# A quantised decoder layer: a lighter prologue, the output codes without GpSimd, power-of-two scales in three steps, and layer norms split with ScalarE

## The reference

```python
# self attention, 16 heads of 64, everything quantised to 8 bits with power-of-two scales
s(t)  = exp2(ceil(log2(max|t| / 127)));  fq_floor(t) = clip(floor(t / s), -128, 127) * s
h     = layernorm(x) * fq_round(gamma) + fq_round(beta)
q,k,v = split(fq_floor(fq_floor(h) @ fq_round(w_qkv)))
dots  = fq_floor(q @ k.T * temp);  attn = fq_floor(softmax(dots))
out   = fq_floor(fq_floor(attn @ v) @ fq_round(w_out))
x1    = layernorm(x + out)                                  # post-norm
# linear cross attention: no softmax, so the context is used only through k.T @ v of each head
x2    = layernorm(x1 + (layernorm(q @ (k.T @ v) * scale + x1) * g + b))
# feed forward: W1, gelu, W2 with affine 8-bit activations and symmetric 8-bit weights
y     = layernorm(x2 + qlinear(gelu(qlinear(x2, W1, b1)), W2, b2))
```

## Time and profile before

| | us |
|---|---|
| three executions | 511.37, 513.91, 508.60 |
| median | 511.37 |
| the profiled execution, its own time | 509.18 |
| its span, from the first to the last instruction | 507.4 |
| around the span | 1.8 |

### The profile page before, as it was taken

How to read it: one execution, slowest core, us unless ns; L and a number is a source line. 1 busy time by engine, 2 the same in 40 slices (tenths; PEclk the granted TensorE clock), 3 DMA queues, 4 the chain that set the end, 5 groups by cost and what they waited for, 6 DMA issues and landing times.

```text
span 507.4 us, 7393 instructions
## 1 busy us (share of the span) xinstructions
PE 251.0 (49%) x1547; PEld 112.7 (22%) x1556; DVE 437.8 (86%) x1429; ACT 332.9 (66%) x739; POOL 174.3 (34%) x333
## 2 busy tenths in 40 slices
PE   0768766877767772222222222209995616405040
PEld 0644221421321211011111111103331614302030
DVE  4995899599769998999999999967775988987967
ACT  1013997299699992899999999954775622516230
POOL 7450000200030000588888888880000804430010
PEclk9976999589955555555555555558999675557557
DMA  7800000000134432188888888783004000000002
GB/s 261 211 2 0 0 0 0 1 21 21 43 116 173 184 146 104 37 191 190 191 189 190 191 188 186 166 165 43 2 1 125 16 1 1 0 1 0 0 1 83
DMA packets 85231, 43.65 MB, mean 86 GB/s; under 512 B 69064, under 2 KB 74456, under 8 KB 85083
## 3 DMA queue, kind: packets, MB, share of 16 engines
q1 hardware_dynamic: 83642, 43.21, 33.3%
q10 hardware_dynamic: 1568, 0.21, 0.3%
HBM read 8.28 MB, written 1.58 MB: 19 GB/s over the span
## 4 chain that ended last, share of the span: by engine, by line
DVE 53%; PE 25%; issue 13%; ACT 5%; DVEq 1%; DMA 1%; POOL 1%; ACTq 0%; SPq 0%
PE ps L476 24%; DVE mem L1176 11%; DVE mem L940 8%; DVE d_max L943 6%; DVE row_max L1176 2%; DVE m L1446 2%; DVE m L1447 2%; DVE mem L1321 2%; DVE mem L1086 1%; ACT mem L847 1%; DMA mem<-in_x 1%; DVE r_now L939 1%; DVE row_code L939 1%; DVE neg_max L939 1%; DVE m L943 1%
## 5 line engine op out<-in xcount | busy, mean ns | idle before, releaser
L476 PE MATMUL ps<-mem 64*128 64x256 bf16 (+6 forms) x1236 | 198.3, 368 | 141.6 <-DMA mem<-mem 83.7
L476 PEld LDWEIGHTS ps<-mem 64*128 64x128 bf16 (+5 forms) x1244 | 83.4, 130 | 252.3 <-issue 169.2
L847 ACT ACTIVATE mem<-mem,neg_max 128x256 f32<-128x256 int16 x256 | 126.3, 494 | 14.0 <-DVE neg_max L939 10.1
L1176 DVE CUSTOM_DVE_ANT_0 mem<-ps,fold,c 128x256 int16<-128x256 f32 x256 | 111.1, 470 | 0.0
L430 POOL TENSOR_SCALAR mem<-mem,r_now 128x256 int16<-128x256 f32 x176 | 80.9, 478 | 72.7 <-DVE r_now L939 72.7
L1086 DVE TENSOR_TENSOR mem<-mem 128x1024 bf16<-128x1024 bf16 x84 | 54.3, 683 | 14.8 <-ACT mem L799 14.7
L799 ACT ACTIVATE mem<-ps,c 128x1024 bf16<-128x1024 f32 x48 | 48.3, 1292 | 1.2 <-PE ps L476 1.2
L847 ACT ACTIVATION_READ_ACCUMULATOR mem<-mem,neg_max 128x1 f32 x256 | 47.8, 187 | 0.0
L813 ACT ACTIVATE mem<-ps,c 128x1024 int16<-128x1024 f32 x32 | 36.0, 1203 | 13.2 <-DVEq L1120 11.9
L940 DVE TENSOR_SCALAR mem<-mem,c 128x2048 bf16<-128x2048 int16 (+3 forms) x43 | 38.0, 895 | 6.4 <-PE ps L476 6.0
L430 POOL TENSOR_SCALAR fine_third<-mem,r_now 128x256 int16<-128x256 f32 x80 | 36.8, 478 | 5.0 <-DVE r_now L939 5.0
(11 more groups left out here) (201 smaller groups left out, 369.8 us busy)
## 6 DMA issues: line engine op xcount, KB each, us to landing
mem<-mem SPq DMA_DIRECT2D x64, 256.0 KB, 2.4
mem<-in_L_attn_w_qkv SPq DMA_DIRECT2D x1, 1536.0 KB, 9.9
mem<-in_L_attn_w_out SPq DMA_DIRECT2D x2, 512.0 KB, 10.8
out<-mem SPq DMA_DIRECT2D x4, 256.0 KB, 2.3
mem<-in_L_ffn_W SPq DMA_DIRECT2D x2, 256.0 KB, 6.0
xattn_matrix<-mem SPq DMA_DIRECT2D x1, 512.0 KB
mem<-xattn_matrix SPq DMA_DIRECT2D x1, 512.0 KB
mem<-mem SPq DMA_TRANSPOSE x22, 4.3
```

What stands on the lines that cost most here:

```text
L476: return te.matmul(o_, l_, r_, start=start, stop=stop)
L847: ins = sc.activation(e_ring[:, u % 4, pos], y_ring[:, u % 4, pos], ACT.Exp, scale=scale_reg, bias=neg_max[:, u % 4, pos:pos + 1], accum_o ...
L1176: ins = ve.tensor_tensor_reduce(y_ring[:, slot, pos], ps[:, 2 * slot + pos // 2, (pos % 2) * N:(pos % 2 + 1) * N], shift, col("g_dots"), - ...
```

## The change

In the prologue, x comes as two halves, the first on SP's queue and the second as the first DMA of ACT's queue, in rows of 1 KB (two neighbouring tokens on a partition; the output is stored the same way). `gbc` follows on ACT's queue, then the bias rows, then the weights. VectorE works out gamma's and beta's codes before the statistics. w_out, W1 and W2 aren't loaded or measured here, but once, late, behind the dots; their maxima, scales, codes and transposes are done between the groups of AV. The context gets a column of ones, so that the Gram matmuls give its sums too and GpSimd adds nothing. h and w_qkv are coded in halves and thirds, and the maximum pass starts with the first of them. `a1`, `r2`, `kv`, `xm` and `xbv` move behind the maximum pass and between units of the code pass, whose loops are written out. AV uses three double banks. `scale_of` works on the fp32 bits in three steps. VectorE reads the last AV pair in PSUM, bank by bank. GpSimd's casts of the output codes go to VectorE. In layer norms 1, 3 and 4 ScalarE normalises two tiles of each quarter, for which VectorE makes `nmr`, minus mean times factor; GpSimd's `x1_beta` waits for all quarters.

```diff
@@ sync: loads @@
-            sp.dma_start(x_in, x.rearrange("b (c p) d -> p (b c) d", p=P)).then_inc(sem("x_loaded"), 16)
+            sp.dma_start(x_in_pairs[:, halves[0]], x_pairs[:, halves[0]]).then_inc(sem("x_first"), 16)
             sp.dma_start(w_qkv_f, w_qkv).then_inc(sem("w_loaded"), 16)
...
-            sp.dma_start(w_out_again, w_out.rearrange("(j p) d -> p j d", p=P)).then_inc(sem("w_out_again"), 16)
+            sp.dma_start(w_out_f, w_out.rearrange("(j p) d -> p j d", p=P)).then_inc(sem("w_late"), 16)
+            sp.dma_start(w1_f, w1.rearrange("(c p) d -> p c d", p=P)).then_inc(sem("w_late"), 16)
+            sp.dma_start(w2_f, w2).then_inc(sem("w_late"), 16)
@@ scalar: loads @@
+            act.dma_start(x_in.rearrange("p (b c) d -> p b (c d)", c=2)[:, B // 2:B],
+                          x.rearrange("b (p c) d -> p b (c d)", c=2)[:, B // 2:B]).then_inc(sem("x_second"), 16)
             act.dma_start(gbc[:, 0:1], at_g[:, None]).then_inc(sem("gb_loaded"), 16)
             act.dma_start(gbc[:, 1:2], at_b[:, None]).then_inc(sem("gb_loaded"), 16)
+            act.dma_start(bkv[:, 0], x_bk[None, :].to_broadcast((B, D))).then_inc(sem("bkv_loaded"), 16)
@@ gpsimd @@
-            for bb in range(B // 2):
-                pool.wait_ge(sem("o_i_act"), bb + 1)
-                pl.tensor_scalar(o_cv[:, bb, 1], o_iv[:, bb, 1], 1.0, 0.0, ALU.mult, ALU.add)\
-                    .then_inc(sem("o_codes_odd"), 1)
@@ tensor: prologue, and between the units of the code pass @@
+            for b in range(4):
+                gram_of(b)
             pe.wait_ge(sem("xw_T"), 1)
+            across(6, diag6[:, 2:3], 1)
+            for b in range(4, 6):
+                gram_of(b)
+            across(0, diag, 1)
+            for b in range(6, B):
+                gram_of(b)
...
+            first = {1: ("hT_codes", 2), 2: ("gram_ready", 2), 3: ("gram_ready", 3), 8: ("w_codes", 3)}
...
+            a1_half(0)
+            across(5, diag, 1)
+            a1_half(1)
...
+                    if n == 4:
+                        pe.wait_ge(sem("a1_ready"), 1)
+                        kv_main(0)
+                    if n == 6:
+                        kv_bias(0)
...
+                    if n == 20:
+                        pe.wait_ge(sem("kv_ready"), 2)
+                        xm_half(0)
@@ vector @@
-                link(ts(t_, grown, factor, TINY * GROW, ALU.mult, ALU.max))
...
+                link(ts(s_out, grown, factor, TINY * GROW * HALF_RANGE, ALU.mult, ALU.max))
+                link(ts(bits, bits, 0x7F800000, None, ALU.bitwise_and))
+                link(ts(inv_out.bitcast(I32), bits, -1.0, float(0x7F000000), ALU.mult, ALU.add))
...
             dve.wait_ge(sem("gb_loaded"), 32)
             link(absmax(m6[:, 0:2], gbc[:].rearrange("p (k n) -> p k n", n=1)))
+            across_send(m6, 2, diag6)
+            across_take(2, 7, x6)
...
+                if grp == 3:
+                    dve.wait_ge(sem("w_late"), 48)
+                    absmax(m6[:, 3:4], w_out_f.rearrange("p j d -> p (j d)")).then_inc(sem("late_max"), 1)
...
+            for k in range(2):
+                dve.wait_ge(sem("av_group"), B * GROUPS - 1 + k)
+                absmax(d_max[:, k:k + 1], ps[:, last_bank + k, :]).then_inc(sem("o_last"), 1)
...
+            for bb in range(B // 2):
+                o_ints(bb)
+                if bb:
+                    o_odd(bb - 1)
+                o_even(bb)
+            o_odd(B // 2 - 1)
...
             def normalise(name, dst, src, q, done):
-                for t in range(4 * q, 4 * q + 4):
+                for t in range(4 * q, 4 * q + 2):
                     ins = norm(dst, src, t)
@@ scalar: layer norms @@
+            def norm_act(name, dst, src, q, done):
+                act.wait_ge(ln_sem(name, "shift"), ln_count(name, q))
+                for t in range(4 * q + 2, 4 * q + 4):
+                    ins = sc.activation(dst[:, t], src[:, t], ACT.Identity, scale=rsd[:, t:t + 1], bias=nmr[:, t:t + 1])
```

559 lines of the change are left out of this document (320 added, 239 removed).

## The result

The changed kernel takes 491.5 us (median of 4 runs, 490.66 to 491.69) against 510.99 for the kernel before (4 runs, 508.6 to 513.91): ratio 0.961, 95% interval 0.956 to 0.967. It is faster by 3.9%. The profiled execution took 491.34 us with a span of 489.4, so by its own time it is 17.8 shorter than the one before (509.18), by the span 18.0. One of the executions that follow, 512.95 us with the third norm on VectorE, ran at a granted clock of 0.58 where its neighbours had 0.68 to 0.70, and no median counts it.

The account below looks back on a forecast made before the run. Streams were taken as bound by two full engines, seams by chains everybody waits on; the change works on seams. Terms 10.0 + 4.0 + 0.9 - 1.5 + 5.7 + 2.5 + 1.3 = 22.9 from 509.18 gave 486.3; stated 487.5, range 478 to 498.

Parts of the forecast that it names:

- Prologue, 10.0: Start to the maximum pass's first matmul: statistics at 15.3, equivalent start at 39.8 instead of 49.83, gain 10.0 us.
- Passes, 4.0: Between, inside and behind the qkv passes: 1.4 + 1.1 - 2.2 - 2.5 + 6.2, gain 4.0 us.
- The term 1.4 for the start: Between the qkv passes: less fp32 work ahead of the exchange, so ScalarE's first code unit comes 1.4 us earlier.
- 1.1 - 2.2 - 2.5: Code pass: ScalarE's gap closed 1.1 us, its added copies cost 2.2, fp32 blocks starving it cost 2.5 (0 to 5).
- Shorter scales, 0.9 for two: Scales for dots and attention: two steps of 0.2 us saved, 0.45 each, gain 0.9 us.
- AV, -1.5: AV: a product of 384 fp32 columns and eight transposes put between TensorE's groups, loss 1.5 us.
- Last pair and output codes, 5.7: After AV: earlier last-pair reduction 0.85 us, scale 0.45 twice, output codes without GpSimd 3.95, gain 5.7.
- Norms 1 to 3, 2.5: Layer norms: first norm 0.8 us, third norm's split and better order before `sum3` 1.7; gain 2.5, between 0 and 5.
- Norm 4, 1.3: Fourth layer norm: 2.0 us less 0.7 at the end, gain 1.3, between 0 and 2.
- a load that isn't held up (481.5): Rival, prologue: `gbc` lands at 4.5, statistics at 9.5, 5.8 us less, 481.5; chance 0.12.
- the clock staying low (531): Rival: new fp32 blocks and late waits keep TensorE at 1.2 GHz through AV and the code pass, 531 us; chance 0.03.
- "Little comes" (495): Rival: GpSimd's products hold VectorE 2.6 us more, fp32 blocks starve the pass 2.5 more, norms give nothing: 495; chance 0.17.

## Why the prediction was right, and where its steps were off

The forecast was 487.5 with a range of 478 to 498; measured 491.5. The sign and the seams were right, and so were the two largest terms, prologue and output codes, within 2 us. The sum was 22.9 where the profiles show 18.0, and it is that near by some luck: four terms fell short by 7.2 in all, three came out 2.3 better. Term by term:

- **Prologue, 10.0: 8.1 came.** The statistics came at 17.45 for 15.3. Of that 1.4 is the load, in at 11.88 for 10.5, held by w_qkv as argued from the earlier trace rows: gamma ahead of w_qkv took 4.0, beta with it 8.4. The other 0.8 is GpSimd's hold, taken at 0.8 and found 1.6 here and up to 3.3, so its upper bound was right. From w_qkv's maximum to the first matmul it was 11.1 us for 11.8; the wait of 2.5 for TensorE in there did not come (the exchange at 33.33 was over while VectorE still reduced `hT`, and that of `hT`'s maximum, ready at 35.37, ran at 35.42). After the first matmul I had added 1.2; by the lead at the pass's end it was 1.8. The prediction had VectorE late to fold, but not that ScalarE would wait for VectorE's semaphore: moving it gave 1.05.
- **Passes, 4.0: 0.35 came.** This is the step that failed. The term 1.4 for the start was -0.6: I shared 7.85 us of fp32 work between both sides of the exchange. Ahead of it stood 5.4 us (79.12 to 84.48) for the 4 assumed, and I overlooked that the far half holds the first code multiplication to 89.32, when the scale is there at 86.8, on a TensorE at half clock. Moving it gave 3.3. Inside, 1.1 - 2.2 - 2.5 was -3.6 and is -5.3; ScalarE's idle time is 4.7, just inside the bound of 5, where 2.5 was taken. Behind the pass 6.2 was right (7.84 before, 1.64 after). By the spread of the code pass the 0.35 is good to about 1 us, which leaves it far from 4.0.
- **Shorter scales, 0.9 for two: 0.4.** The one in front of the softmax gave its 0.45. The attention's brought the codes 0.35 earlier against the exchange, but there VectorE's first conversion for AV, at 332.12, stood beside GpSimd's last probabilities' codes (to 332.59) and took 1.02 us for 0.75; the lead is 8.90 at the softmax and 8.85 at the first AV matmul. GpSimd's hold was not in this term.
- **AV, -1.5: -0.8.** Too dark; why it is half was not tried.
- **Last pair and output codes, 5.7: 6.8** (8.0 to 14.8). The casts on VectorE take 0.68 each as assumed, each issued about 0.6 behind the last, so the codes gained 4.9 for 3.95. GpSimd's leaving is the cause of 4.6 of it, by experiment.
- **Norms 1 to 3, 2.5: 1.4.** Norm 1 gave 1.5 for 0.8, of which 0.9 is the late bias. Norms 2 and 3 gave nothing for 1.7: the split is worth 1.1, and two shifts moved in front of the extremes cost 1.05.
- **Norm 4, 1.3: 1.8.** What it is made of was not tried.

The rivals: a load that isn't held up (481.5) is refuted by its landing; the clock staying low (531) by AV at 1.00 from 344 to 348. "Little comes" (495) had the right causes, GpSimd's holds, the starved pass and norms 2 and 3 without a gain, at other prices: the holds 0.8 more than taken for 2.6, ScalarE's idle time 2.2 more for 2.5, the norms 1.1 less for 2.5. The output casts did speed up.

The rival that held `gbc` behind x but not behind w_qkv would have had the loads in at 7.5 and the statistics at 12.3; they came at 11.88 and 17.45. In the kernel with the small loads first, from 6 to 9.7 us, with w_qkv and then the context on SyncE's queue, the two queues moved packets one for one, and beta's 128 took 8.4 us. The counts also go together in short pieces: in stretches of 0.25 us from 6 to 8.5 they differ by one at most.
```profile
q1 hardware_dynamic: 219, 1.33, 86.6%
q10 hardware_dynamic: 225, 0.10, 10.2%
```

By the Trainium skill (DMA: Bandwidth & Descriptors, section "Queues, rings and completion order") an engine stays with a queue for a whole packet of some 9 to 17 descriptors before it turns to the next. These counts, 219 and 225, which go together piece by piece, disagree (a packet of the profile is one row here: 1.18 MB in 96 packets in the earlier trace rows are w_qkv's rows of 12 KB).

## What to carry to other kernels

A small load on which a long chain hangs goes first on its queue, and ahead of the big load on every other queue: here that was worth 8 us (the first matmul came 7.55 earlier), with GpSimd's products moved to where they hold nothing. Beside GpSimd's products, schedule on VectorE only what isn't held (reductions and norm statistics), and look at the smallest operations when judging such a neighbour: two columns can cost 1.8 us. Work moved into a pass that a third engine paces went in best here as blocks of one bank, spread out (gaps of 0.23 us for 1.09 and 0.71), and worst between an exchange and the first product that waits for it (3.2 us).

## What the runs showed of the hardware that was not expected

- GpSimd holds a VectorE operation to its own end, however small that is: 128x2 fp32 `tensor_scalar` 1.79 us, two 128x4 `scalar_tensor_tensor` 1.31, two diagonals up to 3.80 beside both products, and 2.57 beside a memset. Not held by such neighbours: `bn_stats` (16 in 3.18 us), `tensor_reduce` of the extremes (0.67, with the order changed alone) and of w_qkv (3.34 beside a 2.66 us memset, as without it). The Trainium skill (SBUF — State Buffer, section "Who interferes with whom") has the two engines share one port pair, which the first to issue holds for its whole instruction; on VectorE a `tensor_scalar` or a cast can take it, and two inputs in SBUF need part of it, while a `tensor_reduce` never does. These runs agree, with 1.79 us for the held operation that takes 0.17 alone, and 0.67 for the reduction.
- The start of the hold is a matter of 0.1 us. In the eight profiled executions with that part unchanged the products began between 12.0 and 12.4 us, and cost 1.6 us in four and 3.0 to 3.3 in four. In the first four VectorE's two diagonals had begun 0.06 to 0.27 us ahead of the first product, in the others they began 0.02 to 0.34 behind it and were held by both. The first matmul came at 39.8 to 40.0 in the first four and at 41.4 to 41.5 in the others: nearly all of the difference between one execution's prologue and another's.
